# Two unused products in front of each of row units 12 to 23 of the first quad

## The reference

```python
x = x + lru(layernorm(x))                  # complex state of 64 channels, scanned over 1024 positions
z = layernorm(x)
h = z + attention(rmsnorm(z, ln1))         # softmax(q k^T / sqrt(8)) v, 16 heads, 4 batches of 1024 rows
h = h + moe(rmsnorm(h, ln2))               # top 2 of 8 experts: silu(a w1) * (a w3), then w2
out = x + h
```

## Time and profile before

| | us |
|---|---|
| median of 3 runs | 1009.26 |
| lowest, highest | 1009.2, 1010.88 |
| the profiled execution | 1012.09 |
| its span | 1010.3 |
| TensorE (PE) busy | 869.8 |
| VectorE (DVE) busy | 847.7 |
| ScalarE (ACT) busy | 694.2 |
| GpSimd (POOL) busy | 401.5 |

### The profile page before, as it was taken

The page is one execution under the profiler, slowest core; times in us unless marked ns, Lnnn a source line. Parts: engine busy times, 40 slices in busy tenths (PEclk is TensorE's granted clock), DMA queues, the critical chain, the costliest instruction groups (busy, mean ns, idle before and its releaser), DMA issues.

```text
span 1010.3 us, 18276 instructions
## 1 busy us (share of the span) xinstructions
PE 869.8 (86%) x5968; PEld 362.6 (36%) x5968; DVE 847.7 (84%) x1441; ACT 694.2 (69%) x1482; POOL 401.5 (40%) x621
## 2 busy tenths in 40 slices
PE   0377788999999999999999999999999988889991
PEld 0155542222222222222222222222322234689990
DVE  4978889999999998988999898898799963677664
ACT  2614312888888888888888888888788876545660
POOL 7223351010010153523715444363577402347774
PEclk9789996999999999999999999999999999989996
DMA  9997543010110110100100010110101011123346
GB/s 313 387 355 196 140 128 94 9 25 17 24 25 10 29 28 9 46 9 26 36 27 25 9 46 10 32 46 10 25 31 40 20 35 36 44 60 92 102 150 195
DMA packets 60829, 74.34 MB, mean 74 GB/s; under 512 B 9152, under 2 KB 39104, under 8 KB 60352
## 3 DMA queue, kind: packets, MB, share of 16 engines
q1 hardware_dynamic: 53936, 62.93, 20.9%
q0 software_dynamic: 4608, 9.58, 2.8%
q10 hardware_dynamic: 2192, 0.66, 0.3%
HBM read 28.09 MB, written 44.79 MB: 72 GB/s over the span
## 4 chain that ended last, share of the span: by engine, by line
PE 57%; DVE 23%; ACT 8%; issue 5%; POOL 3%; ACTq 1%; DMA 1%; POOLq 0%; DVEq 0%; SPq 0%
PE ps L1633 20%; DVE nmax L1202 12%; PE ps L1623 9%; PE ps L1521 8%; ACT prob L961 7%; PE ps L1735 7%; PE ps L1751 3%; PE ps L1510 2%; PE ps L1696 2%; PE ps L1497 1%; DVE wk L1152 1%; ACTq L836 1%; PE ps L1656 1%; POOL by_expert_rows L731 1%; PE ps L1715 1%
## 5 line engine op out<-in xcount | busy, mean ns | idle before, releaser
L1202 DVE TENSOR_REDUCE nmax<-ps 128x1 f32<-128x1024 f32 x512 | 602.0, 1220 | 43.4 <-PE ps L1521 39.1
L961 ACT ACTIVATE prob<-ps 128x512 f32<-128x512 f32 x1024 | 528.4, 603 | 85.6 <-PE ps L1623 84.5
L1521 PE MATMUL ps<-packs 50*128 50x512 bf16 x1024 | 343.0, 389 | 9.5 <-DVE nmax L1202 5.4
L1623 PE MATMUL ps<-packs 50*128 50x512 bf16 x1024 | 311.8, 384 | 36.4 <-ACT prob L961 27.1
L1633 PE MATMUL ps<-prob,vpad 128*32 128x512 f32 x2048 | 273.6, 606 | 0.0
L1521 PEld LDWEIGHTS ps<-packs 50*128 50x128 bf16 x1024 | 74.7, 93 | 240.2 <-DVE nmax L1202 184.7
L1623 PEld LDWEIGHTS ps<-packs 50*128 50x128 bf16 x1024 | 75.9, 93 | 155.1 <-ACT prob L961 105.8
L544 POOL MEMSET packs<- 2x2048 bf16 x32 | 57.5, 1797 | 170.7 <-PE ps L1623 169.5
L810 POOL DMA_INDIRECT by_token<-wk,vall x80 | 80.3, 1003 | 101.2 <-DVE wk L1292 57.1
L1735 PE MATMUL ps<-ws 128*128 128x128 f32 x640 | 87.6, 281 | 3.6 <-DVE ws L1312 3.1
L1735 PEld LDWEIGHTS ps<-ws 128*128 128x128 f32 x640 | 79.4, 195 | 10.6 <-issue 9.8
(11 more groups left out here) (300 smaller groups left out, 852.0 us busy)
## 6 DMA issues: line engine op xcount, KB each, us to landing
by_expert_rows<-prob SPq DMA_DIRECT2D x4, 5016.0 KB, 36.8
packs<-k_parts SPq DMA_DIRECT2D x32, 192.0 KB, 3.5
packs<-q_parts SPq DMA_DIRECT2D x64, 96.0 KB, 3.0
vall<-by_expert_rows SPq DMA_DIRECT2D x80, 66.0 KB
packs<-by_token SPq DMA_DIRECT2D x8, 512.0 KB, 5.0
w<-w_t SPq DMA_DIRECT2D x3, 1024.0 KB, 10.5
q_parts<-front SPq DMA_DIRECT2D x16, 192.0 KB, 3.0
k_parts<-front SPq DMA_DIRECT2D x16, 192.0 KB, 3.4
```

The source lines that it names most:

```text
L961: act.activation(prob[:, v % RING, :], bank(col_bank(pos)), ACT.Exp).then_inc(col_free, 1)
L1202: dve.tensor_reduce(nmax[:, half, par, pair, qt:qt + 1], bank(first, 2), AX_X, ALU.max, negate=True).then_inc(row_free, 1)
L1521: ins = pe.matmul(bank(first + kh), qpack[r:r + ROWS, slot, half, pair, qt * P:(qt + 1) * P], kpack[r:r + ROWS, slot, pair, kh * HALF:(kh ...
L1623: pe.matmul(bank(col_bank(pos)), kpack[r:r + ROWS, slot, head // 2, kt * P:(kt + 1) * P], qpack[r:r + ROWS, slot, half, head // 2, :], sta ...
```

## The change

`unused_products` gets a second argument, the bank that it writes, and `score_unit` a number of unused products. With a number, `score_unit` waits for the pair of the unit to be free, which is the wait that `score_row` makes anyway, then writes the unused products into the first 256 columns of the pair's first bank, and then the unit's own two products overwrite them. All calls for units 12 to 23 pass 2; the calls in `last_half` stay as they are. The kernel's result is the same.

```diff
+            def unused_products(n, to=0):
+
+                for _ in range(n):
+                    pe.matmul(ps[:, to, 0:2 * P], ident16[:, :], ident[:, :].bitcast(BF16), start=True, stop=True)
+
-            def score_unit(p):
+            def score_unit(p, unused=0):
 
+                if unused:
+                    pe.wait_ge(row_free, pair_pos(p, True) - 1)
+                    unused_products(unused, to=row_unit(p, True)[4])
                 for kh in range(2):
                     score_row(p, kh, 0, 0, opening=True)
...
-            def unused_products(n):
-
-                for _ in range(n):
-                    pe.matmul(ps[:, 0, 0:2 * P], ident16[:, :], ident[:, :].bitcast(BF16), start=True, stop=True)
...
             for p in range(12, 16):
-                score_unit(p)
+                score_unit(p, unused=2)
             pe.wait_ge(rest_left, 2 * B + 2)
             pe.wait_ge(v_saved, B)
-            score_unit(16)
-            score_unit(17)
+            score_unit(16, unused=2)
+            score_unit(17, unused=2)
             turn_maxima(0, 0)
             for p in range(18, LEAD):
-                score_unit(p)
+                score_unit(p, unused=2)
```

## The result

The changed kernel is slower: median 1014.56 us of 10 runs (1010.53 to 1015.42) against 1010.99 us for the kernel before (10 runs, 1009.14 to 1012.8), a ratio of 1.0032 with a 95% interval of 1.0020 to 1.0045. The forecast of 1007.5 us was on the wrong side, and its range ended at 1011.4. Of the distance of 7.1 us, 3.6 is the change; 1.8 is the gain that was forecast, and 1.7 is that the median of before moved from 1009.26 (3 runs) to 1010.99 (10).

What follows compares the result with a forecast made beforehand. It took VectorE's row maxima to bound the row units, and TensorE at the low clock groups 0 and 1. Gains of 0.35 and 1.5 us, together 1.8, took 1009.26 to 1007.5 us; range over all cases 1006.0 to 1011.4.

Steps and rivals of the forecast that it cites:

- What bounds the kernel: First quad's row units: VectorE's reductions set the pace, 1.13 us apart, 1.18 at the low clock; groups 0 and 1 take 6.3.
- The price at 2.4 GHz: Units 12 to 23: two unused products cost 0.32 us a unit, hidden behind VectorE; 0 to 0.3 us on the path.
- Will the clock stay up?: Units 12 to 23 up to group 2: the clock leans to holding at 1.00, with little certainty; chance 0.48.
- rival 1: Row units: clock falls all the same near 159 us, unused products on the path, 1.5 to 2.2 us lost, 1011.1; chance 0.27.
- What holding would bring: Up to group 2: 0.35 us from some 8 units and 1.5 from groups 0 and 1 (4.8 for 6.3), together 1.8 us.
- rival 2: Clock holds for the units and falls in group 0; only the units' 0.35 us stays, 1008.9 us; chance 0.13.
- The forecast's base: Whole kernel: median of the runs shown, 1009.26 us, from which the saving was taken; those runs differ by 1.7 us.

Runs made afterwards that it cites:

- e3_four_50rows: e1_four with the four unused products of each of units 12 to 23 over 50 rows, not 128: 1013.73 us, ratio 1.0038 to the kernel before.
- e2_three: The changed kernel with three unused products over all rows ahead of each of units 12 to 23, not two: 1015.67 us, ratio 1.0051 to the kernel before.
- e1_four: The changed kernel with four unused products over all rows ahead of each of units 12 to 23, not two: 1013.95 us, ratio 1.0029 to the kernel before.
- g1_two_of_512: The changed kernel with its two unused products over all rows of 512 columns each, not 256: 1014.28 us, ratio 1.0025 to the kernel before.
- e4_four_group0: e1_four plus six unused products over all rows in group 0 of the first quad: 1009.52 us, ratio 0.9986 to the kernel before.

## Why the prediction was wrong

**What bounds the kernel.** Right, for before: VectorE's 1.13 us at the upper level, nearly so at the lower, and 6.3 us for groups 0 and 1.

**The price at 2.4 GHz.** Right: 0.32 us forecast for two unused products, 0.32 measured; units still 1.13 us apart.

**"Will the clock stay up?"** This is the step that failed. The prediction set the changed unit between a stretch that holds and one that falls and chose the first "because the clock is up when the change sets in". That was no reason: the clock was up ahead of before's fall as well. It also took busy time as the measure, while two rows that it had itself cited pointed elsewhere: 8.99 of 10.60 us busy with 50-row products that did not bring the clock back, against 4.94 of 8.00 us busy with 128-row products at 1.00. In its place the runs showed that the clock falls at 157.9 us though TensorE is busy 2.59 of 3.40 us. `e3_four_50rows`, `e2_three` and `e1_four` show that the rows of the products matter, and `e1_four` and `g1_two_of_512` that two products of 256 columns are too little work. The section "A second HAM failure mode: psum-queue depth-cycling" in "TensorE: Matmul & The Clock Gate" of the Trainium skill names short idles as a cause of such falls, and the changed kernel's trace agrees: it falls with idles of 0.20 and 0.40 us. But short idles are not the whole cause either, since `e1_four` holds with idles of 0.19 us as well. By which rule the clock decides stays open.

**The size of rival 1.** The case was foreseen, with 0.27, at 1.5 to 2.2 us; it measured 3.15. Two terms were too small. The pitch was worked out as half of a cycle in which TensorE waits for the reduction two units back, 1.39 to 1.49 us. In fact TensorE doesn't wait at all: two unused and two own products in line take 0.54 + 0.96 = 1.50 us, and that is the bound. And seven units were counted (3.5 cycles), where the fall is ahead of unit 15 and nine are left to unit 23; the earlier trace rows have 19 products between 159.0 and 169.6 us, those of nine units and `turn_maxima`'s. 9 x (1.51 - 1.18) = 3.0 us; the rest, some 0.1, is in groups 0 and 1.

**What holding would bring.** Right in size for groups 0 and 1: 6.35 - 4.83 = 1.52 us by `e4_four_group0` for 1.5. But neither profile of the changed kernel has it with two products, and holding the units alone doesn't bring it: group 0 has to be held too. That rival 2 "gives 1008.9" was too kind. When the clock falls in group 0 and not earlier, it comes back later as well, and the opening is 1.8 to 1.9 us longer, not 0.35 shorter. Some 0.7 us of that is the price of the greater work ahead of the units; the other 1.1 to 1.2 us is the later low stretch.

**The forecast's base.** The three runs shown were on the low side; the bounds of the range should have allowed for a kernel whose runs lie 5 us apart.

## What to carry to other kernels

Filler products are safe only if they keep the clock up. At 2.4 GHz, behind another engine's bound, two per unit were free and four cost 0.7 us in all; if the clock falls in spite of them, they run at 1.2 GHz on the path. So price them first at the lower clock, as TensorE's whole time per unit against the other engine's pitch, and use as many as hold the clock or none. Follow the clock past the stretch that is filled, up to where TensorE has enough work of its own; and look for the single long wait of TensorE elsewhere in the kernel, which was cheaper to fill here than the many short ones. Judge such a change by the stretch that it touches, since the runs as a whole scatter more than it moves them.

## What the runs showed of the hardware

- Of two kernels in which TensorE runs the same number of equally long products, the clock fell in the one with 50-row products (busy 2.83 of 3.40 us ahead of the fall) and held in the one with 128-row products (14.66 of 16.70 us). With three 128-row products, busy 2.82 of 3.40 us, it held in the place where the 50-row kernel's fell.
- Being busy does not bring the clock back by itself: the changed kernel has TensorE busy 13.50 of 13.50 us at 0.50.
- A switch between products over 50 and over all 128 rows takes time: at the lower clock the pair of 512 columns took 0.96 us until the next product over all rows, where two steps of such products are 2 x (1.03 - 0.60) = 0.86 (two take 1.03, one alone 0.60), and this with TensorE never idle. Products over 50 rows of different halves of the partitions overlapped instead: two units with eight unused products stood 3.21 us apart in `e3_four_50rows`, where eight times 512 columns in line would be 8 x 0.43 = 3.44.
- The runs of one kernel differ with the time that they spend at the lower clock. Runs of before on the chip of the last experiments with a mean granted clock of 0.970 took 1007.5 to 1008.4 us, those with 0.965 to 0.966 took 1010.9 to 1012.8. Filling one wait of 2.70 us brought a spread of 5.7 us (31 runs, 1007.25 to 1012.99) down to 3.0 (12 runs, 1005.94 to 1008.97).
- The same idle times can bring a fall in one execution and none in another: TensorE waits 1.55 and 1.11 us just ahead of 88 us in the profiles of before and of `e1_four`, in the same work, and the clock is 0.50 after it in the first and 1.00 in the second. Why was not tried. Nor was filling the low stretches ahead of 120 us tried; before has one of 17 us from 39.5 us on and three short ones.
